# Nine quarters of the key projection inside the first three steps, and the opening loads on three queues

## The chip, the cores and the metric

One program on one core of a Trainium2 chip. The metric is the device time in microseconds (us); lower is better. The kernel before took 767.0, 773.41 and 774.11 us in three runs, median 773.41 us.

## The reference, cut to what matters

One post-norm decoder block over x of shape (32, 128, 256), float32: causal self-attention with 16 heads, a cross attention without softmax (rotated queries and keys, a decay mask), and a mixture of 8 experts of which each token uses two, with a shared expert. The part that this change touches is how the self-attention gets its keys:

```python
qkv = jnp.einsum('bsd,de->bse', x, qkv_weights).reshape(-1, 3 * D)
q = jnp.transpose(pre_q, (0, 2, 1, 3)).reshape(-1, S, Dh)
v = jnp.transpose(pre_v, (0, 2, 1, 3)).reshape(-1, S, Dh)
k = jnp.transpose(pre_k, (0, 2, 3, 1)).reshape(-1, S, Dh)   # k is reshaped across positions
a = jnp.einsum('aib,ajb->aij', q, k) / scale
a = jax.nn.softmax(tril * a + NEG_INF * (1.0 - tril), axis=-1)
x = _layernorm(x + heads)            # then cross attention, norm, experts, norm
```

The reshape of k mixes positions and channels, so the keys of a head aren't a slice of the projection: the kernel writes the projected keys to a DRAM tensor, k_dram, and reads them back in another order.

## The kernel before, in words

**The key projection.** x is 32 batches, taken as 4 groups of 8. For each group the projection of K comes in 4 quarters, so there are 16 quarters. A quarter (project_k, line 711) is four float32 products of 256 columns, eight records in the trace, into one PSUM bank; VectorE then copies the bank into first_use (out_k, line 1242). After four quarters SyncE stores the group, 1 MB, to k_dram (store_k, line 445). The rows of a group lie batch by batch: batch b of a group is 16 of the 128 partitions. Before the loop TensorE does 12 quarters (line 720), then waits for every load of the opening (lines 728 to 735); the last four come in steps 0 and 1 (lines 846 to 851 and 935 to 938), each behind a wait on kk_set, the count of copied quarters.

**The loop.** Each engine runs step(n) for n from -2 on, one batch further in each stage per step. In step n TensorE turns the probabilities of batch n-1 in four pieces (turn_probs, line 778), applies them to v of batch n-2 (weigh), makes the scores of batch n (scores, line 761), and projects q and v of batch n+1 (project, line 737). VectorE takes the row maxima (line 1259), lays the causal mask of two of the four score banks for the next batch (line 1365), and does the moments of the norms. ScalarE does the exponentials (line 1085), copies the turned probabilities out (line 1092), lays the other two masks (line 1097) and scales q (line 1149). Each engine does its own in the order written; semaphores order them against each other. scores(n) needs q, the four masks (near_laid, far_laid) and the keys of batch n (kp_in).

**SyncE's queue.** All loads of the opening are issued by SyncE in one row: wk (the K part of the weights), group 0 of x in four pieces, groups 1 to 3, the identity, the Q and V weights, and then load_small (line 435): gate and shared biases, the tables tf and tb (the mask is in tb), and the three cross attention weights. Then store_k(0), and in the loop per step: x for the next projection (line 470), the keys of batch n+1 in eight reads of 16 KB (line 480), one store_k, context and rows of x (lines 501, 505). In steps 3 to 6 it also loads the experts' weights into first_use (lines 488 to 497), ahead of the context of that step. GpSimd's queue writes zeros for idle rows to sent in step 2 (line 627), as soon as zeros is set.

## Time and profile before

| | |
|---|---|
| median of three runs | 773.41 us |
| the profiled execution, whole time | 769.79 us |
| its span, first to last instruction | 768.0 us |
| granted TensorE clock, mean over the span | 0.971 |
| TensorE busy | 702.7 us (92%) |
| first scores of the loop begin | 32.51 us into the span |

The profiled execution is one of its own. Its 769.79 us are the span and 1.8 us around it. Times of rows below count from the span's start. A row of the timeline gives start, duration, engine, line and operation, and in brackets how long the engine had been idle before it and what ended that. The profile's granted clock is 1.00 at TensorE's upper level (2.4 GHz) and 0.50 at its lower (1.2 GHz).

### The profile page before, as it was taken

What the parts mean: (1) busy time and instruction counts of PE and PEld (TensorE: products, weight loads), DVE (VectorE), ACT (ScalarE), POOL (GpSimd) and SP (SyncE); (2) the same over time, 40 slices, a digit from 0 to 9 for tenths busy, and PEclk for the clock granted to TensorE, in tenths of its full rate; (3) what the DMA queues carried; (4) which work ended last, traced back from release to release, by engine and by line L of the source; (5) the groups of instructions that cost most, each with busy time, mean ns of one, the idle gap of its engine ahead of it and who ended that gap; (6) DMA issues with size and microseconds to landing.
All of it is one profiled execution on the core that took longest, in us unless ns stands there. A gap on an engine that the chain in (4) does not pass through costs nothing.

```text
span 768.0 us, 19404 instructions
## 1 busy us (share of the span) xinstructions
PE 702.7 (92%) x5464; PEld 531.7 (69%) x5465; DVE 479.0 (62%) x1536; ACT 409.2 (53%) x1167; POOL 333.8 (43%) x483
## 2 busy tenths in 40 slices
PE   6977899999999999999987649999999999999993
PEld 5866788888888888888875315566666666665453
DVE  3555577888888888888865433444444444438984
ACT  0268688888888888888851102333333333312232
POOL 1002233345555555555565553555555555541111
PEclk9999999999999999999999768999999999999998
DMA  8745562223333332333371543322222222218962
GB/s 296 249 146 155 149 220 75 82 65 101 102 90 90 101 112 77 102 101 98 91 235 53 155 138 117 125 89 83 89 82 89 82 89 82 89 59 319 307 213 82
DMA packets 77032, 97.54 MB, mean 127 GB/s; under 512 B 12320, under 2 KB 63264, under 8 KB 75936
## 3 DMA queue, kind: packets, MB, share of 16 engines
q1 hardware_dynamic: 59920, 68.21, 28.5%
q0 software_dynamic: 6816, 19.00, 6.9%
q10 hardware_dynamic: 10224, 9.42, 4.6%
q8 instruction: 39, 0.64, 0.4%
q14 instruction: 33, 0.27, 0.1%
HBM read 60.02 MB, written 36.56 MB: 126 GB/s over the span
## 4 chain that ended last, share of the span: by engine, by line
PE 69%; issue 13%; DVE 4%; POOL 4%; SPq 4%; DMA 4%; ACT 1%; DVEq 0%; POOLq 0%; ACTq 0%
PE ps L996 16%; PE ps L1007 8%; PE ps L783 6%; PE ps L861 4%; PE ps L771 4%; PE ps L793 4%; PE ps L748 4%; PE ps L864 3%; PE ps L885 3%; PE ps L751 3%; DVE products L1269 3%; PE ps L982 2%; POOL sent L640 2%; PE ps L989 2%; PE ps L922 2%
## 5 line engine op out<-in xcount | busy, mean ns | idle before, releaser
L1085 ACT ACTIVATE prob<-ps,nmax 128x128 f32<-128x128 f32 x512 | 146.4, 377 | 29.1 <-DVE nmax L1259 29.0
L996 PE MATMUL ps<-first_use,xgT 128*128 x284 | 135.6, 600 | 1.5 <-ACT xgT L1190 1.5
L1489 DVE TENSOR_TENSOR hid<-ps,attn_only 128x512 f32<-128x512 f32 x71 | 49.1, 692 | 95.6 <-PE ps L996 94.4
L1190 ACT COPY xgT<-ps 128x256 f32<-128x256 f32 x71 | 26.4, 372 | 137.2 <-PE ps L982 137.2
L1259 DVE TENSOR_REDUCE nmax<-ps 128x4 f32<-128x512 f32 x128 | 82.2, 685 | 19.9 <-PE ps L771 18.5
L677 POOL TENSOR_TENSOR gate_h<-hid,sil 128x256 f32<-128x256 f32 x71 | 50.8, 715 | 96.6 <-DVE result_row L1502 83.0
L1092 ACT COPY pT<-ps 128x512 f32<-128x512 f32 x128 | 76.7, 599 | 18.9 <-PE ps L783 14.7
L783 PE MATMUL ps<-tf,prob 128*128 128x128 f32 x512 | 78.2, 275 | 5.7 <-ACT pT L1092 5.7
L996 PEld LDWEIGHTS ps<-first_use,xgT 128*128 128x128 f32 x284 | 54.3, 192 | 40.5 <-issue 37.0
L640 POOL DMA_INDIRECT sent<-packets,pos x64 | 63.7, 995 | 37.3 <-PE ps L771 22.8
L680 POOL DMA_INDIRECT back<-yg,result_row x71 | 71.5, 1007 | 14.3 <-issue 12.4
L1007 PE MATMUL ps<-first_use,ghT 128*128 x284 | 74.1, 384 | 0.5 <-ACT ghT L1195 0.5
L783 PEld LDWEIGHTS ps<-tf,prob 128*128 128x128 f32 x512 | 59.2, 141 | 11.8 <-issue 5.8
L801 PE MATMUL ps<-prob,sw_sb 128*128 128x512 f32 x128 | 62.7, 641 | 3.5 <-DMA prob<-x2T_dram 2.5
L647 POOL TENSOR_TENSOR res<-att,attn_only 128x256 f32<-128x256 f32 x32 | 23.4, 731 | 86.9 <-DVE att L1387 86.9
L1508 DVE TENSOR_TENSOR yg<-ps,attn_only 128x256 f32<-128x256 f32 x71 | 30.2, 425 | 41.7 <-PE ps L1007 37.6
L982 PEld LDWEIGHTS ps<-tf,xg 128*128 128x128 f32 x142 | 18.8, 143 | 52.3 <-issue 50.9
L621 POOL TENSOR_TENSOR rot<-products 128x128 f32<-128x128 f32 x128 | 54.2, 455 | 0.0
L1007 PEld LDWEIGHTS ps<-first_use,ghT 128*128 128x128 f32 x284 | 48.4, 190 | 4.9 <-issue 0.9
L1269 DVE TENSOR_TENSOR products<-ps,tf 128x256 f32<-128x256 f32 x128 | 46.3, 404 | 5.0 <-PE ps L864 1.1
L801 PEld LDWEIGHTS ps<-prob,sw_sb 128*128 128x128 f32 x128 | 25.7, 205 | 32.9 <-issue 29.5
L659 POOL TENSOR_TENSOR rstd<-mv,neg_half 128x1 f32<-128x1 f32 x32 | 17.6, 550 | 67.0 <-DVE mv L1277 67.0
(135 smaller groups left out, 1408.8 us busy)
## 6 DMA issues: line engine op xcount, KB each, us to landing
xg<-sent ACTq DMA_DIRECT2D x68, 129.5 KB, 2.1
first_use<-back SPq DMA_DIRECT2D x8, 1024.0 KB, 7.9
k_dram<-first_use SPq DMA_DIRECT2D x4, 1024.0 KB, 4.4
attn_only<-in_x_turned SPq DMA_DIRECT2D x32, 128.0 KB, 3.0
attn_only<-k_dram SPq DMA_DIRECT2D x256, 16.0 KB
attn_only<-in_x SPq DMA_DIRECT2D x32, 128.0 KB, 2.8
attn_only<-in_ctx SPq DMA_DIRECT2D x32, 128.0 KB, 2.9
first_use<-in_L_ffn_rw SPq DMA_DIRECT2D x8, 512.0 KB, 5.2
```

The lines of the kernel that those rows point to most:

```text
L621: eng.tensor_tensor(rot[:, t % 2, m + e, :], ra[:, t % 2, m + e, :], rb[:, t % 2, m + 1 - e, :], ALU.add).then_inc(done, 1)
L640: eng.indirect_dma_start(sent, bass.IndirectOffsetOnAxis(ap=pos[:, t, j:j + 1], axis=0), packets[:, t % SLOTS, :], None).then_inc(sent_in[ ...
L677: eng.tensor_tensor(gate_h[:, r, :], hid[:, r, FFN:2 * FFN], sil[:, r, :], ALU.mult).then_inc(gh_set, 1)
L680: eng.indirect_dma_start(back, bass.IndirectOffsetOnAxis(ap=result_row[:, slot:slot + 1], axis=0), yg[:, slot % 2, :], None).then_inc(yg_o ...
L783: mm = eng.transpose(PROBT[:, n * P:(n + 1) * P], prob[:, t % 2, 4 * u + n, :], ident)
L801: mm = eng.matmul(ps[:, bank0 + 2 * f + half, :].rearrange("p (b t) -> p b t", b=QB), sw1_sb[:, c, cols:cols + P], x2T4[:, r, :, c, :], st ...
L996: mm = eng.matmul(ps[:, r, :], xgT[:, r, c, :], rw1_sb[:, bass.ds(e * (DC * 2 * FFN) + c * 2 * FFN, 2 * FFN)], start=(c == 0), stop=(c == ...
L1007: mm = eng.matmul(ps[:, 4 + r, 0:D], ghT[:, r, c, :], rw2_sb[:, bass.ds(e * (FFN // P * D) + c * D, D)], start=(c == 0), stop=(c == FFN // ...
L1085: ins = eng.activation(prob[:, t % 2, 4 * u + n, :], SCORE[u][:, n * P:(n + 1) * P], ACT.Exp, bias=nmax[:, t % 2, 4 * u + n:4 * u + n + 1])
L1092: eng.copy(pT[:, u, :, :].rearrange("p n t -> p (n t)"), PROBT).then_inc(pT_set, 1)
L1259: eng.tensor_reduce(nmax[:, t % 2, 4 * u:4 * u + 4], SCORE[u].rearrange("p (h j) -> p h j", j=P), AX_X, ALU.max, negate=True).then_inc(max ...
L1269: eng.tensor_tensor(into[:, t % 2, m:m + 2, :], source, table[:, m:m + 2, :], ALU.mult).then_inc(done, 1)
```

## The change

What it does, by place:

- TensorE does quarters 0 to 3 first, then the projection of q and v of batch 0 and the masks, then quarters 4 to 6, then the first scores. Quarters 7 to 9 lie in step 0, 10 to 12 in step 1, 13 to 15 in step 2. A table, K_BANK, gives each quarter its PSUM bank. VectorE's copies follow (out_ks).
- The big wait ahead of the loop is split: tables and cross weights are waited for in step 3, the small ones in step 5.
- SyncE loads only the K weights, group 0, the Q and V weights, x for batches 0 and 1, tb and the identity. ScalarE's queue loads group 1 (when group 0 is in), group 2 (in step 0) and group 3 (behind its first four exponentials). GpSimd's queue does load_small, when group 1 is in.
- The store of group 0 is two stores: the 16 partitions of batch 0, and the other 112. Batch 0's keys are then read by SyncE (four reads) and ScalarE (four reads).
- Stores of groups 1 to 3 come at the end of SyncE's steps 0 to 2; experts' weights one step later (steps 4 to 7); the zeros in GpSimd's step 4.

```diff
 MAX_ORDER = (1, 0, 3, 2)
+K_BANK = (4, 5, 6, 7, 4, 5, 7, 4, 5, 7, 5, 7, 5, 7, 6, 7)
 PADDING = B * S * TOPK
...
         kk_set = sem("kk_set")
-        k_stored = [sem("k_stored_first"), sem("k_stored_rest")]
+        k_stored = [sem("k_stored_batch"), sem("k_stored_group"), sem("k_stored_rest")]
+        mask_in = sem("mask_in")
...
                               x_blocks[0, :, 2 * j:2 * j + 2].rearrange("p u n -> p (u n)")).then_inc(first_in[j], 16)
-            for g in range(1, NG):
-                eng.dma_start(xTu[g][:, :, :, :, :].rearrange("p u c b i -> p (u c b i)"),
-                              x_blocks[g].rearrange("p u n -> p (u n)")).then_inc(xTu_in[g], 16)
-            eng.dma_start(ident, table_f32[:, 0:P]).then_inc(ident_in, 16)
             for n in (0, 2):
                 eng.dma_start(wqkv_sb[:, :, n * D:(n + 1) * D], wqkv_rows[:, :, n * D:(n + 1) * D]).then_inc(w_in, 16)
-            def load_small():
-                eng.dma_start(gate_w_sb[:, :, :], gate_w.rearrange("(c p) n -> p c n", p=P)).then_inc(small_in, 16)
...
-                eng.dma_start(tb[:, :], table_bf16).then_inc(tables_in, 16)
-                for w, src in ((xwq_sb, xwq), (xwk_sb, xwk), (xwv_sb, xwv)):
-                    eng.dma_start(w[:, :, :], src.rearrange("(c p) n -> p c n", p=P)).then_inc(xw_in, 16)
+            eng.dma_start(xT[:, 0, :, :], x_turned[0]).then_inc(xT_in[0], 16)
+            eng.dma_start(tb[:, :], table_bf16).then_inc(mask_in, 16)
+            eng.dma_start(xT[:, 1, :, :], x_turned[1]).then_inc(xT_in[1], 16)
+            eng.dma_start(ident, table_f32[:, 0:P]).then_inc(ident_in, 16)
...
                 eng.wait_ge(kk_set, g * 4 + 4)
-                eng.dma_start(k_dram[g * GB:(g + 1) * GB].rearrange("b i g f -> (b i) (g f)"),
-                              kk_of(g)).then_inc(k_stored[min(g, 1)], 16)
-            load_small()
+                rows = k_dram[g * GB:(g + 1) * GB].rearrange("b i g f -> (b i) (g f)")
+                if g == 0:
+                    eng.dma_start(rows[0:DH, :], kk_of(g)[0:DH, :]).then_inc(k_stored[0], 16)
+                    eng.dma_start(rows[DH:P, :], kk_of(g)[DH:P, :]).then_inc(k_stored[1], 16)
+                else:
+                    eng.dma_start(rows, kk_of(g)).then_inc(k_stored[2], 16)
             store_k(0)
...
                 t = n + 2
-                if live(t):
+                if live(t) and t > 1:
                     after(eng, qv_made, t - 1)
...
                         eng.wait_ge(consts_set, 2)
-                    if t == 0:
-                        eng.wait_ge(k_stored[0], 16)
-                    for j in range(GB):
+                    if t < 2:
+                        eng.wait_ge(k_stored[t], 16)
+                    for j in range(GB if t else GB // 2):
                         lo = 16 * j
...
                                       k_dram[t, :, j, :]).then_inc(kp_in[t % 2], 16)
-                if n in (-1, 0, 1):
-                    store_k(n + 2)
-                if n == 3:
-                    eng.wait_ge(k_stored[1], 16 * (NG - 1))
-                if 2 < n <= 2 + NE // 2:
-                    if n == 3:
+                if n == 4:
+                    eng.wait_ge(k_stored[2], 16 * (NG - 1))
+                if 3 < n <= 3 + NE // 2:
+                    if n == 4:
                         eng.dma_start(sw1_sb[:, :, :], sw1[0].rearrange("(c p) n -> p c n", p=P)).then_inc(ffn_in, 16)
...
-                    for e in range(2 * (n - 3), 2 * (n - 2)):
+                    for e in range(2 * (n - 4), 2 * (n - 3)):
                         lo = e * DC * 2 * FFN
...
                     eng.dma_start(xn[:, t % 2, :], x[t]).then_inc(xn_in[t % 2], 16)
+                if n in (0, 1, 2):
+                    store_k(n + 1)
                 if n == B:
...
+            def load_small():
+                eng.dma_start(tf[:, P:], table_f32[:, P:]).then_inc(tables_in, 16)
+                for w, src in ((xwq_sb, xwq), (xwk_sb, xwk), (xwv_sb, xwv)):
+                    eng.dma_start(w[:, :, :], src.rearrange("(c p) n -> p c n", p=P)).then_inc(xw_in, 16)
+                eng.dma_start(gate_w_sb[:, :, :], gate_w.rearrange("(c p) n -> p c n", p=P)).then_inc(small_in, 16)
+                eng.dma_start(gate_b_sb[:, 0:NE], gate_b.rearrange("(o n) -> o n", o=1).broadcast_to([P, NE])).then_inc(small_in, 16)
+                eng.dma_start(sb1_sb[:, :], sb1[0].rearrange("(c p) -> p c", p=P), allow_slow_non_contiguous=True).then_inc(small_in, 16)
+                eng.dma_start(sb2_sb[:, :], sb2.broadcast_to([P, D])).then_inc(small_in, 16)
+            eng.wait_ge(xTu_in[1], 16)
+            load_small()
             def turn_into(t, m, made, done):
...
             def step(n):
-                if n == 2:
+                if n == 4:
                     eng.wait_ge(zeros_set, 1)
...
-            for g in range(NG - 1):
-                eng.wait_ge(xTu_in[g] if g else wk_in, 16)
-                for j in range(4):
-                    if g == 0:
-                        eng.wait_ge(first_in[j], 16)
-                    else:
-                        eng.wait_ge(kk_set, (g - 1) * 4 + j + 1)
-                    project_k(g, j, 4 + j)
-            eng.wait_ge(xTu_in[NG - 1], 16)
-            eng.wait_ge(ident_in, 16)
+            def project_ks(first, end):
+                for i in range(first, end):
+                    if i == 0:
+                        eng.wait_ge(wk_in, 16)
+                    if i < 4:
+                        eng.wait_ge(first_in[i], 16)
+                    elif i % 4 == 0:
+                        eng.wait_ge(xTu_in[i // 4], 16)
+                    if K_BANK[i] in K_BANK[:i]:
+                        eng.wait_ge(kk_set, i - K_BANK[:i][::-1].index(K_BANK[i]))
+                    project_k(i // 4, i % 4, K_BANK[i])
+            project_ks(0, 4)
             eng.wait_ge(w_in, 32)
-            eng.wait_ge(kk_set, 4 * NG - 5)
-            eng.wait_ge(tables_in, 32)
-            eng.wait_ge(xw_in, 48)
-            eng.wait_ge(small_in, 64)
+            eng.wait_ge(mask_in, 16)
             eng.wait_ge(consts_set, 2)
+            eng.wait_ge(kk_set, 3)
...
             def step(n):
+                if n == 0:
+                    project_ks(4, 7)
                 if n == 1:
-                    eng.wait_ge(kk_set, 13)
+                    eng.wait_ge(ident_in, 16)
+                    eng.wait_ge(kk_set, 8)
+                if n == 3:
+                    eng.wait_ge(tables_in, 16)
+                    eng.wait_ge(xw_in, 48)
+                if n == 5:
+                    eng.wait_ge(small_in, 64)
                 if live(n - 1):
...
                 if n == 2:
-                    eng.wait_ge(kk_set, 4 * NG)
+                    eng.wait_ge(kk_set, 13)
                 if live(n - 2):
...
                 if n == 0:
-                    eng.wait_ge(kk_set, 9)
-                    project_k(NG - 1, 0, 4)
+                    project_ks(7, 9)
                 if n == 1:
-                    eng.wait_ge(kk_set, 14)
-                    project_k(NG - 1, 3, 5)
+                    project_ks(10, 11)
+                if n == 2:
+                    project_ks(13, 14)
                 t = n - 3
...
                     turn_probs(n - 1, 1)
+                if n == 1:
+                    project_ks(11, 12)
                 t = n - 3
...
                     turn_probs(n - 1, 2)
+                if n == 1:
+                    project_ks(12, 13)
+                if n == 2:
+                    eng.wait_ge(q_set, 3)
+                    eng.wait_ge(v_set, 3)
+                    project_ks(14, 16)
                 t = n - 5
...
                     mm.then_inc(gate_made, 1)
+                if n == 2:
+                    eng.wait_ge(kk_set, 15)
                 if live(n + 1):
...
                 if n == 0:
-                    eng.wait_ge(kk_set, 12)
-                    project_k(NG - 1, 1, 5)
-                    project_k(NG - 1, 2, 7)
+                    project_ks(9, 10)
                 for q in groups_at(n, 3):
...
                     eng.wait_ge(x1_set, t + 1)
+                    if n == 2:
+                        eng.wait_ge(kk_set, 4 * NG)
                     after(eng, gc_set, n - 4)
...
+            def load_blocks(g):
+                eng.dma_start(xTu[g][:, :, :, :, :].rearrange("p u c b i -> p (u c b i)"),
+                              x_blocks[g].rearrange("p u n -> p (u n)")).then_inc(xTu_in[g], 16)
+            eng.wait_ge(first_in[3], 16)
+            load_blocks(1)
             def step(n):
+                if n == 0:
+                    load_blocks(2)
+                    eng.wait_ge(k_stored[0], 16)
+                    for j in range(GB // 2, GB):
+                        lo = 16 * j
+                        eng.dma_start(kp[lo:lo + DH, 0, j % 2, :, :].rearrange("p a u -> p (a u)"),
+                                      k_dram[0, :, j, :]).then_inc(kp_in[0], 16)
                 if live(n - 1):
...
                     exps(n, 1)
+                if n == 0:
+                    load_blocks(3)
                 for q in groups_at(n, 1):
...
         def _(eng):
-            def out_k(g, j, bank):
-                eng.wait_ge(k_made, g * 4 + j + 1)
-                eng.tensor_copy(kk_of(g).rearrange("p (a u) -> p u a", u=NU)[:, 2 * j:2 * j + 2, :],
-                                ps[:, bank, :].rearrange("p (u a) -> p u a", u=2)).then_inc(kk_set, 1)
-            for g in range(NG - 1):
-                for j in range(4):
-                    out_k(g, j, 4 + j)
-            eng.wait_ge(tables_in, 32)
-            eng.wait_ge(consts_set, 2)
-            eng.tensor_copy(base[:, :], region_rows).then_inc(base_set, 1)
-            eng.tensor_copy(zeros[:, D:PACKET], padding_end).then_inc(zeros_set, 1)
+            def out_ks(first, end):
+                for i in range(first, end):
+                    eng.wait_ge(k_made, i + 1)
+                    eng.tensor_copy(kk_of(i // 4).rearrange("p (a u) -> p u a", u=NU)[:, i % 4 * 2:i % 4 * 2 + 2, :],
+                                    ps[:, K_BANK[i], :].rearrange("p (u a) -> p u a", u=2)).then_inc(kk_set, 1)
+            out_ks(0, 4)
...
                 r2, r4 = t2 % 2, t4 % 2
+                if n == 0:
+                    out_ks(4, 7)
+                    eng.wait_ge(mask_in, 16)
+                    eng.wait_ge(consts_set, 2)
+                if n == 1:
+                    out_ks(9, 10)
                 if live(n):
...
                 if n == 0:
-                    for j, bank in enumerate((4, 5, 7)):
-                        out_k(NG - 1, j, bank)
+                    out_ks(7, 9)
                 if n == 1:
-                    out_k(NG - 1, 3, 5)
+                    out_ks(10, 12)
+                if n == 2:
+                    out_ks(13, 14)
                 if live(t2):
...
                                       rden[:, r2, :].unsqueeze(2).broadcast_to([P, H, DH]), ALU.mult).then_inc(att_set, 1)
+                if n == 2:
+                    out_ks(14, 15)
                 if live(t3):
...
                     lay_mask(n + 1, 3)
+                if n == 1:
+                    out_ks(12, 13)
+                if n == 2:
+                    out_ks(15, 16)
+                    eng.wait_ge(tables_in, 16)
+                    eng.tensor_copy(base[:, :], region_rows).then_inc(base_set, 1)
+                    eng.tensor_copy(zeros[:, D:PACKET], padding_end).then_inc(zeros_set, 1)
                 if live(t4):
```

TensorE's order from its first product to scores(1), before (714 is a quarter's product, four to a quarter; 748 and 751 the projection of q and v, 758 the masks, 771 the scores, 783 turned probabilities):

```order
L714 MATMUL ps<-attn_only,prob 128x256 x32
L714 MATMUL ps<-attn_only,first_use 128x256 x16
L748 MATMUL ps<-attn_only 128x128 x4
L751 MATMUL ps<-attn_only 128x256 x2
L758 MATMUL ps<-tb 128x512 x4
L771 MATMUL ps<-attn_only 128x128 x16
L714 MATMUL ps<-attn_only,first_use 128x256 x4
L748 MATMUL ps<-attn_only 128x128 x4
```

and now (721 is a quarter's product, 757 and 760 the projection, 767 the masks, 780 the scores, 792 turned probabilities; lines of the changed file):

```order
L721 MATMUL ps<-attn_only,prob 128x256 x16
L757 MATMUL ps<-attn_only 128x128 x4
L760 MATMUL ps<-attn_only 128x256 x2
L767 MATMUL ps<-tb 128x512 x4
L721 MATMUL ps<-attn_only,prob 128x256 x12
L780 MATMUL ps<-attn_only 128x128 x16
L721 MATMUL ps<-attn_only,prob 128x256 x4
L721 MATMUL ps<-attn_only,first_use 128x256 x4
L757 MATMUL ps<-attn_only 128x128 x4
L760 MATMUL ps<-attn_only 128x256 x2
L721 MATMUL ps<-attn_only,first_use 128x256 x4
L792 MATMUL ps<-tf,prob 128x128 x4
```

Twelve quarters stood ahead of the first scores and seven do now; the projection and the masks have moved in among them. Quarter 8, the first from first_use, needs group 2.

VectorE in step 2, from the maxima of batch 2 to the masks for batch 3, before (1365 is the mask, 1244 would be a quarter's copy):

```order
L1259 TENSOR_REDUCE nmax<-ps 128x4 [waits expd,scored] x3
L1382 RECIPROCAL rden<-ps 128x16 [waits heads_turned]
L1387 TENSOR_TENSOR att<-ps,rden 128x256 [waits den_set]
L1396 BN_STATS bn<-res 128x6 [waits res1_set]
L1273 BN_AGGR mv<-bn 128x2 [waits bn1_set]
L1277 TENSOR_SCALAR mv<-mv 128x1 [waits mv1_set]
L1259 TENSOR_REDUCE nmax<-ps 128x4 [waits expd,scored]
L1411 TENSOR_SCALAR x<-res,mv,rstd 128x256 [waits rstd1_set]
L1365 CAST ps<-tb 128x512 [waits expd] x2
```

and now (1288 is a quarter's copy, 1402 the mask):

```order
L1296 TENSOR_REDUCE nmax<-ps 128x4 [waits expd,scored] x3
L1288 COPY first_use<-ps 128x2x256 [waits k_made]
L1426 RECIPROCAL rden<-ps 128x16 [waits heads_turned]
L1431 TENSOR_TENSOR att<-ps,rden 128x256 [waits den_set]
L1288 COPY first_use<-ps 128x2x256 [waits k_made]
L1442 BN_STATS bn<-res 128x6 [waits res1_set]
L1310 BN_AGGR mv<-bn 128x2 [waits bn1_set]
L1314 TENSOR_SCALAR mv<-mv 128x1 [waits mv1_set]
L1296 TENSOR_REDUCE nmax<-ps 128x4 [waits expd,scored]
L1457 TENSOR_SCALAR x<-res,mv,rstd 128x256 [waits rstd1_set]
L1402 CAST ps<-tb 128x512 [waits expd] x2
L1288 COPY first_use<-ps 128x2x256 [waits k_made]
```

Three copies now lie in this step, the last behind both masks; TensorE's transposes of x1 (line 987 of the changed file), which stand at the end of its step 2, wait for that last copy.

## Rows read from the trace of the kernel before

**Rows 1.** The page: shares of the chain that ended last, by engine
```profile
PE 69%; issue 13%; DVE 4%; POOL 4%; SPq 4%; DMA 4%; ACT 1%; DVEq 0%; POOLq 0%; ACTq 0%
```

**Rows 2.** Timeline, 0 to 60 us, up to the first scores
```profile
5.78 16.49 PE L714 MATMUL ps<-attn_only,prob 128*128 128x256 f32 x64 [5.78 <-DMA prob<-in_x_blocks]
...
15.40 1.08 DVE L1244 COPY first_use<-ps 128x512 f32<-128x512 f32 x1 [0.65 <-PE ps L714]
17.12 1.08 DVE L1244 COPY first_use<-ps 128x512 f32<-128x512 f32 x1 [0.65 <-PE ps L714]
...
29.01 1.10 PE L748 MATMUL ps<-attn_only 128*128 128x128 f32 x8
...
30.81 1.03 PE L758 MATMUL ps<-tb 128*128 128x512 bf16 x4
...
32.51 1.17 PE L771 MATMUL ps<-attn_only 32*128 32x128 f32 x32 [0.67 <-DMA attn_only<-k_dram]
```

**Rows 3.** Chain that ended last, 0 to 80 us: start, duration, what
```profile
19.17 8.32 DMA k_dram<-first_use
...
30.73 1.64 DMA attn_only<-k_dram
...
71.16 7.78 DMA attn_only<-in_ctx
```

**Rows 4.** Stretches: start:end, length, each engine's busy us, granted clock, DMA share, GB/s
```profile
19.00:26.00 7.00, 7.00 (x35) 6.16 (x34) 4.43 (x5) 0.00 (x0) 0.00 (x0) 1.00 0.94 353
32.50:43.36 10.86, 8.74 (x72) 7.65 (x73) 6.82 (x9) 6.50 (x21) 0.00 (x0) 1.00 0.90 300
43.36:54.51 11.15, 9.61 (x101) 7.80 (x101) 4.85 (x7) 7.56 (x23) 0.00 (x0) 0.85 0.38 124
44.90:48.10 3.20, 3.20 (x10) 2.47 (x9) 2.30 (x5) 2.17 (x8) 0.00 (x0) 0.50 0.03 8
54.50:64.60 10.10, 6.85 (x102) 5.75 (x98) 5.52 (x12) 8.66 (x26) 1.30 (x2) 1.00 0.22 55
```

**Rows 5.** Timeline, steps 0 to 2: TensorE, VectorE, ScalarE
```profile
33.71 2.49 DVE L1259 TENSOR_REDUCE nmax<-ps 128x4 f32<-128x512 f32 x4 [3.36 <-PE ps L771]
...
41.77 1.34 DVE L1365 CAST ps<-tb 128x512 f32<-128x512 bf16 x2
...
43.36 1.17 PE L771 MATMUL ps<-attn_only 32*128 32x128 f32 x32 [2.12 <-DVE ps L1365]
...
54.51 1.18 PE L771 MATMUL ps<-attn_only 32*128 32x128 f32 x32
...
59.26 0.63 PE L783 MATMUL ps<-tf,prob 128*128 128x128 f32 x4 [2.34 <-ACT pT L1092]
...
63.56 0.60 ACT L1097 CAST ps<-tb 128x512 f32<-128x512 bf16 x1
...
64.64 1.17 PE L771 MATMUL ps<-attn_only 32*128 32x128 f32 x32
```

**Rows 6.** Timeline: SyncE's and GpSimd's DMA issues, 31 to 68 us
```profile
31.04 1.15 POOL L627 DMA_DIRECT2D sent<-zeros  x1 [27.50 <-DVE zeros L1254]
31.19 0.42 SPq L447 DMA_DIRECT2D k_dram<-first_use  x1
...
32.13 6.79 SPq L480 DMA_DIRECT2D attn_only<-k_dram  x8
...
63.44 4.64 SPq L480 DMA_DIRECT2D attn_only<-k_dram  x8
```

**Rows 7.** Line 447, the four stores of K, issue to landing
```profile
DMA to landing us min/median/max: 4.2/4.4/8.3
```

**Rows 8.** Line 429, loads of groups 1 to 3, issue to landing
```profile
DMA to landing us min/median/max: 8.1/10.1/12.2
```

**Rows 9.** Timeline of TensorE: context products of batch 0 and of batch 1
```profile
65.74 1.16 PE L861 MATMUL ps<-attn_only 128*128 128x128 f32 x8
...
78.98 2.08 PE L861 MATMUL ps<-attn_only 128*128 128x128 f32 x8 [2.60 <-DMA attn_only<-in_ctx]
```

More of the change, by code:

```diff
@@ L427, in _ @@
                               x_blocks[0, :, 2 * j:2 * j + 2].rearrange("p u n -> p (u n)")).then_inc(first_in[j], 16)
-            for g in range(1, NG):
-                eng.dma_start(xTu[g][:, :, :, :, :].rearrange("p u c b i -> p (u c b i)"),
-                              x_blocks[g].rearrange("p u n -> p (u n)")).then_inc(xTu_in[g], 16)
-            eng.dma_start(ident, table_f32[:, 0:P]).then_inc(ident_in, 16)
             for n in (0, 2):
                 eng.dma_start(wqkv_sb[:, :, n * D:(n + 1) * D], wqkv_rows[:, :, n * D:(n + 1) * D]).then_inc(w_in, 16)
-            def load_small():
-                eng.dma_start(gate_w_sb[:, :, :], gate_w.rearrange("(c p) n -> p c n", p=P)).then_inc(small_in, 16)
-                eng.dma_start(gate_b_sb[:, 0:NE], gate_b.rearrange("(o n) -> o n", o=1).broadcast_to([P, NE])).then_inc(small_in, 16)
-                eng.dma_start(sb1_sb[:, :], sb1[0].rearrange("(c p) -> p c", p=P), allow_slow_non_contiguous=True).then_inc(small_in, 16)
-                eng.dma_start(sb2_sb[:, :], sb2.broadcast_to([P, D])).then_inc(small_in, 16)
-                eng.dma_start(tf[:, P:], table_f32[:, P:]).then_inc(tables_in, 16)
-                eng.dma_start(tb[:, :], table_bf16).then_inc(tables_in, 16)
-                for w, src in ((xwq_sb, xwq), (xwk_sb, xwk), (xwv_sb, xwv)):
-                    eng.dma_start(w[:, :, :], src.rearrange("(c p) n -> p c n", p=P)).then_inc(xw_in, 16)
```

## The prediction, as it was made

> **What bounds the kernel now.** The page comes first: TensorE makes up 69% of the chain of work that ended last [rows 1], so a microsecond that TensorE loses at the start is lost at the end, and one that it gains there is gained, as long as the steps behind it keep their pace. The timeline of the opening is next [rows 2]. TensorE starts on the quarters of K at 5.78 us; VectorE's copies of quarters 3 and 4 start 1.72 us apart (15.40 and 17.12), and that is the pace of a quarter. The projection of q and v for batch 0 starts at 29.01 us, behind twelve quarters, the masks end at 31.84, and the first scores start at 32.51 after 0.67 us of waiting for keys. The chain of waits shows a second path that is almost as long: the store of group 0, issued at 19.17 although its last copy ended at 16.48 (15.40 plus 1.08), takes 8.32 us, and the last key read issued at 30.73 takes 1.64 us more [rows 3]. TensorE's queue and the DMA path end within 0.7 us of each other, so a change has to shorten both.
>
> Then the steps. Between the first scores and 64.6 us TensorE isn't full [rows 4]: it is idle for 2.12 us in the first of the three stretches (10.86 less 8.74), 1.54 in the second, 3.25 in the third, 6.9 together. The gap of 2.12 us stands ahead of scores(1) and ends with VectorE's mask [rows 5]. About 1.5 us after it the granted clock is at the lower of its two levels, 1.2 GHz, from 44.9 to 48.1 us [rows 4]; 3.2 us at half rate cost 1.6. A gap of 2.34 us at 59.26 [rows 5] has no such fall behind it: that stretch is at 1.00 throughout [rows 4].
>
> **What the change can win at most.** TensorE does the same sixteen quarters. The gain can only be idle time or low clock that goes away: 0.67 + 6.9 + 1.6 = 9.2 us up to scores(3), which stand at 64.64 us [rows 5].
>
> **The first scores.** TensorE: quarter 3 is made at 15.4, the projection and the masks take 2.8 us (29.01 to 31.84, of which the projection 1.8) [rows 2], three quarters 5.2, so TensorE is ready at 23.4. Group 1 for quarter 4 is needed at 18.2; in the trace it landed 8.1 us after its issue at 3.2 us, behind 1.3 MB [rows 8]. It now starts some 5 us later with about 1 MB beside it, and should be in by 14: no cost.
>
> The keys: the store of batch 0's 16 partitions can start at 16.5 to 16.9, since load_small no longer stands ahead of it (2.7 us of issue before). Its landing is not in the trace; the bounds are 1.64 us, the key read, and 8.3, the slowest of the 1 MB stores [rows 3, 7], with 4.2 for an undisturbed 1 MB store. I take 3, between the small read and that 4.2: 19.6. Four reads on each queue need 1.4 us to the last issue, 21.0. Their landing has the bounds 1.64 and 7.78, the latter the context read behind a row of bulk loads [rows 3]. Here they stand behind the other 0.9 MB of group 0's store on one queue and behind 1 MB of group 2 on the other, while GpSimd's loads drain. In flight from 17.5 on are about 0.9 + 1.05 + 0.8 MB; at 353 GB/s, the rate of the stretch from 19 to 26 us in which the DMA engines were 94% busy [rows 4], that is 7.8 us, to 25.3. I take 4 us for the reads: first scores at **25.0**, TensorE idle for 1.6 us ahead of them.
>
> The Trainium skill (DMA: Bandwidth & Descriptors, Issuing engines are not separate DMA queues) says that loads issued from several engines run on the same 16 DMA engines, and that spreading them saves only the issue time. Taken alone it would leave the keys where the bytes put them and give this part only the 2.7 us of earlier issue; the 0.94 share agrees with it. The order of the bytes, which the change also turns, is outside that rule.
>
> **Steps 0 to 2.** Step 0 has the same work on TensorE as before (scores, three quarters, the projection, one turned piece), 8.74 us [rows 4]. VectorE has the scores' 1.2, four maxima (2.5), two copies (2.2) and two masks (1.3) [rows 5], and ends 7.2 after the scores began; before, a third copy stood ahead of the masks, and it had to wait for its quarter. ScalarE with its extra issues needs about 8. So scores(1) at 33.7, with no gap where 2.12 us were. Step 1 had 9.61 busy [rows 4]; less 1.6 for the low clock and 1.7 for its one quarter that is 6.3, with three quarters, 5.2, it is 11.5, less a few tenths that each piece's end overlaps with the next once no gap stands between them: 10.8. The quarters lie in the places where TensorE waited for ScalarE's copies. scores(2) at 44.5. Step 2: 6.85 of work [rows 4] plus three quarters, 5.2, is 12.0; two waits stay. The third turned piece waits about 1 us for ScalarE (the same place had 2.34, of which quarter 13 now covers the rest). At the end, x1 is transposed only when quarter 15 has been copied, and that copy of 1.08 stands behind both masks on VectorE; ScalarE then needs 0.4 for x1, 0.6 for its own mask [rows 5] and 0.4 for q before scores(3). In the old order TensorE's project ran into this point; now it waits about 1.3. Step 2 is 14.3, scores(3) at 58.8 against 64.64: 5.8 us. The other way of counting, 9.2 less the 1.6, 1.0 and 1.3 that wait now, is 5.3. I take **5.6**.
>
> VectorE's mask no longer makes TensorE wait, and I expect no low clock in step 1: 1.6 of the 5.6 are that.
>
> **What comes later.** Experts' weights move from step 3 to step 4. They cost a stall: the context of batch 1 is read behind them and lands 7.78 us after its issue [rows 3], TensorE waits 2.60 us and then runs slowly (2.08 us for products that take 1.16 elsewhere) [rows 9]. The same queue order one step later gives the same stall one step later: nothing gained or lost. New beside it are the zeros (0.93 MB) on GpSimd's queue, which start in step 4 as soon as GpSimd is free. In the trace, the eight key reads issued next to zeros and a store took 6.79 us, in step 3 without either 4.64 [rows 6]. So the context comes 0 to 2.15 us later; I take 0.9, as the zeros start some microseconds ahead of the reads. SyncE's store of group 3 now makes it wait in step 2 for quarter 15, about 2 us past the moment at which it would have loaded x for batch 5; that load is not needed for a step: no cost, and if the cover went it would be 2 us. VectorE's two small copies, 0.3 us, lie ahead of a wait. Nothing else moves.
>
> **The sum.** 5.6 less 0.9 is 4.7 us. Against the profiled execution that is 769.8 - 4.7 = 765.1; that execution is 3.6 us under the median of 773.4, which would give 768.7. The three runs and the profiled one average 771.1, so neither is typical; I forecast **767**. About 1%, 7.7 us, is what a measurement of this kernel can tell from no change.
>
> **Rivals.**
> - *The keys are early* (0.20). The store lands in 2 us and the reads behind it in 2: first scores at 23.4, TensorE never waits. Then 5.6 + 1.6, and 0.3 more if the zeros cost little: 7.5, about 764. For it: batch 0's store is an eighth of a group. Against it: the busy DMA engines.
> - *The bytes decide* (0.20). All three queues drain together and the keys land at 28; TensorE is idle for 4.6 us and, as behind the 2.12 us gap, runs at the low clock afterwards: 3.0 and 1.6 lost, gain about 0, 771.
> - *Group 2 is late* (0.09). It is issued at about 18.2, when ScalarE has q and v of batch 0, and quarter 8 wants it at 27.8. If it lands after the longest time seen, 12.2 us [rows 8], it comes at 30.4: 2.6 us lost, gain 2, 769.
> - *Slower* (0.06). Batch 0's store stands behind GpSimd's 1.6 MB as group 0's store stood behind the same loads, 8.3 us, so 25.2; the reads then take 7.78: first scores at 34.4, against 32.51. This turns the sign from 30.6 on (25.0 + 5.6). Price: 9.4 less 5.6, and 1.6 for the clock, 5.4 slower, 777. Against it: those loads are on another queue now.
>
> **Chances.** The forecast itself has 0.45, with a range of its own of 764 to 770. Faster by over 1%: all of the first rival and about 0.12 of the forecast's, whose base may as well be the 770 of the profile: 0.32. Slower by over 1%: 0.06. Within 1%: 0.62. Range: 761 takes in the early keys, 773 the bytes' case and the scatter between runs (767.0 to 774.1); what is left out is the slow rival and the ends of the scatter.
>
> **What the new profile would show.** First scores near 25 us, ahead of them a gap of 1 to 2 us that ends with a DMA (over 4: the bytes; none: early keys). scores(1), (2), (3) near 33.7, 44.5, 58.8. Granted clock 1.00 through step 1; 0.50 behind the first scores would cost 1.6. In step 2 a gap ahead of the turned x1, ended by VectorE's copy of quarter 15; if it isn't there, the gain at scores(3) is 7. In step 5 a gap of 2.6 to 4.7 ended by the context's DMA; if it is gone, the forecast is 4 us too high. From step 6 on each step as before.

## The result, and the profile after

The changed kernel takes 774.31 us (median of 22 runs, 768.0 to 777.98), the kernel before on the same chip 769.74 (22 runs, 765.41 to 775.24). The ratio is 1.0055, with a 95% interval of 1.0035 to 1.0075: by this ratio 4.2 us slower, where 4.7 us less were forecast. The profiled execution of after took 772.58 us, with a span of 770.8, against the 768.0 of before.

The opening of the changed kernel, from its timeline (start, duration, engine, line, operation, tiles; in brackets the idle time ahead of it and what ended it):

```profile
14.25 0.77 POOL L612 DMA_DIRECT2D tf<-in_table_f  x1 [10.71 <-DMA prob<-in_x_blocks]
16.24 0.34 SPq L441 DMA_DIRECT2D k_dram<-first_use  x1
16.62 0.42 SPq L442 DMA_DIRECT2D k_dram<-first_use  x1
16.89 0.35 ACTq L1127 DMA_DIRECT2D first_use<-in_x_blocks  x1
...
21.61 2.01 ACTq L1139 DMA_DIRECT2D attn_only<-k_dram  x4
21.66 1.91 SPq L475 DMA_DIRECT2D attn_only<-k_dram  x4
30.05 2.09 PE L780 MATMUL ps<-attn_only 32*128 32x128 f32 x32 [7.17 <-DMA attn_only<-k_dram]
...
40.49 1.17 PE L780 MATMUL ps<-attn_only 32*128 32x128 f32 x32
51.49 1.17 PE L780 MATMUL ps<-attn_only 32*128 32x128 f32 x32
```

TensorE is ready for the first scores 9.0 us earlier than in [rows 2], at 22.9 instead of 31.84 us, but the keys let the first scores start only at 30.05, 2.5 us earlier than before. The batch's store is issued at 16.24, and the reads, which wait for it, start at 21.6. The table of DMA issues from 14 to 30 us (tile, queue, transfers, KB, median us from issue to landing) shows how long everything in flight then takes:

```profile
first_use<-in_x_blocks ACTq DMA_DIRECT2D x1, 1024.0 KB, 11.4
k_dram<-first_use SPq DMA_DIRECT2D x1, 896.0 KB, 10.5
tf<-in_table_f POOLq DMA_DIRECT2D x1, 705.0 KB, 4.7
k_dram<-first_use SPq DMA_DIRECT2D x1, 128.0 KB, 5.3
```

Group 2's 1 MB needs 11.4 us where the fastest store of that size took 4.2 [rows 7]. The chain of waits has the store and the last read one behind the other:

```profile
16.24 5.34 DMA k_dram<-first_use
23.16 6.76 DMA attn_only<-k_dram
...
84.14 7.78 DMA attn_only<-in_ctx
```

The stretches of the opening (start:end, length, busy time of PE, PEld, DVE, ACT, POOL, then granted clock, DMA share, GB/s), to be read against [rows 4]:

```profile
17.00:21.50 4.50, 4.50 (x23) 3.78 (x21) 1.38 (x2) 0.53 (x2) 2.75 (x5) 1.00 0.99 331
21.50:27.00 5.50, 1.39 (x7) 0.88 (x5) 1.85 (x2) 0.00 (x0) 0.00 (x0) 1.00 1.01 373
27.00:30.00 3.00, 0.00 (x0) 0.00 (x0) 0.00 (x0) 0.00 (x0) 0.00 (x0) 0.50 0.40 95
30.00:33.20 3.20, 3.15 (x35) 2.77 (x36) 0.92 (x2) 0.19 (x1) 0.00 (x0) 0.50 0.10 24
33.20:33.80 0.60, 0.60 (x3) 0.51 (x2) 0.60 (x2) 0.60 (x4) 0.00 (x0) 0.50 0.00 0
```

The DMA engines are full for ten microseconds, 3.5 MB in 17 to 27 us, and fall to 95 GB/s just before the keys are in. The clock is at 1.2 GHz from 27.0 to 33.8 us; the scores take 2.09 us in place of 1.17. Step 0, from these scores to the next, takes 10.44 us (30.05 to 40.49) for work of 8.74 us [rows 4], with no gap: the low clock costs 1.7 us.

Steps 2 and 5, later in TensorE's timeline:

```profile
63.78 0.41 PE L987 MATMUL ps<-tf,x 128*128 128x128 f32 x2 [1.26 <-DVE first_use L1288]
65.59 1.17 PE L780 MATMUL ps<-attn_only 32*128 32x128 f32 x32
...
91.96 2.08 PE L878 MATMUL ps<-attn_only 128*128 128x128 f32 x8 [3.78 <-DMA attn_only<-in_ctx]
103.55 1.17 PE L780 MATMUL ps<-attn_only 32*128 32x128 f32 x32
```

scores(3) start at 65.59 against 64.64 [rows 5]: +1.0 us. The wait for batch 1's context is 3.78 us against 2.60 [rows 9], so scores(6) are at 103.55 against 101.47: +2.1. The last batch's scores are at 383.05 against 380.79, +2.3, and the spans differ by 2.8.

### The profile page after: what moved, and what is told of

It reads as the page before. It is cut to its first block, busy times and chain, and to the rows that moved or that the text cites. A ratio compares the mean times of both kernels' runs of the same rounds, so it can differ in the third digit from the quotient of the medians.

```text
span 770.8 us, 19409 instructions
## 1 busy us (share of the span) xinstructions
PE 702.1 (91%) x5464; PEld 531.3 (69%) x5465; DVE 478.2 (62%) x1536; ACT 410.0 (53%) x1167; POOL 339.3 (44%) x491
## 4 chain that ended last, share of the span: by engine, by line
PE 70%; issue 14%; DVE 5%; POOL 4%; DMA 4%; SPq 1%; ACT 1%; ACTq 0%; POOLq 0%; DVEq 0%
PE ps L1023 16%; PE ps L1034 8%; PE ps L792 5%; PE ps L780 5%; PE ps L878 4%; PE ps L802 4%; PE ps L757 4%; PE ps L881 3%; PE ps L904 3%; PE ps L760 3%; PE ps L721 3%; DVE products L1306 3%; PE ps L1009 2%; POOL sent L647 2%; PE ps L1016 2%
## 5 line engine op out<-in xcount | busy, mean ns | idle before, releaser
L654 POOL TENSOR_TENSOR res<-att,attn_only 128x256 f32<-128x256 f32 x32 | 23.4, 730 | 97.9 <-DVE att L1431 97.9
L1009 PEld LDWEIGHTS ps<-tf,xg 128*128 128x128 f32 x142 | 18.8, 143 | 53.1 <-issue 51.7
```

## The experiments

Each kernel is `after` with the edit shown, except the one built on `before`. A ratio is to the kernel before, timed on the same chip. The chips differ (the kernel before has medians from 769.7 to 776.4 us on them), and so do two openings of the same code, so rows of different traces are compared only roughly.

**Which of the three bulk transfers holds the keys.** First, GpSimd's loads wait for the keys:

```diff
-            eng.wait_ge(xTu_in[1], 16)
+            eng.wait_ge(kp_in[0], 128)
             load_small()
```

> The changed kernel, with GpSimd's 1.6 MB of tables and weights loaded only when batch 0's keys are in. Theory 1 (the keys land when the bytes queued on the 16 DMA engines ahead of them have drained): 1.6 MB less at 373 GB/s is 4.3 us, so the first scores come near 26 us instead of 30.05, with no or less low clock behind them, and the kernel takes 4 to 6 us less than the changed one, about 769 to 771. Rival (the reads of freshly stored keys are slow by themselves, whatever else is in flight): first scores stay at 29 to 30, time unchanged near 774.

Second, group 2 is issued right behind group 1:

```diff
             load_blocks(1)
+            load_blocks(2)
             def step(n):
                 if n == 0:
-                    load_blocks(2)
```

> The changed kernel, with group 2 loaded by ScalarE's queue right behind group 1, into the quiet stretch from 11 to 17 us (221 and 86 GB/s) instead of at 16.9 us. Theory 1: 1.05 MB less beside the keys, 2.8 us: first scores near 27.2, 3 to 4 us less than the changed kernel. Rival: first scores at 29 to 30, time as the changed kernel.

Third, the rest of group 0 is stored behind SyncE's four reads of batch 0:

```diff
                 if g == 0:
                     eng.dma_start(rows[0:DH, :], kk_of(g)[0:DH, :]).then_inc(k_stored[0], 16)
-                    eng.dma_start(rows[DH:P, :], kk_of(g)[DH:P, :]).then_inc(k_stored[1], 16)
...
+                if n == -1:
+                    rows = k_dram[0:GB].rearrange("b i g f -> (b i) (g f)")
+                    eng.dma_start(rows[DH:P, :], kk_of(0)[DH:P, :]).then_inc(k_stored[1], 16)
```

> The changed kernel, with the store of group 0's other 112 partitions (0.92 MB) issued behind SyncE's four reads of batch 0's keys. Theory 1: SyncE's four reads land 3 us or more sooner, ScalarE's four still stand behind group 2 on their own queue but with less traffic beside them: first scores at 27.5 to 29. Batch 1's keys come later by some 5 us and may then hold up scores(1). Rival: no change of the first scores.

The fourth kernel has all three edits.

> All three together: GpSimd's loads behind batch 0's keys, group 2 right behind group 1, the rest of group 0's store behind batch 0's reads. Theory 1: nothing large is in flight when the keys are stored and read; store lands in 2 to 3 us, reads in 2, TensorE hardly waits: first scores at 22.9 to 24.5, granted clock 1.00 behind them, scores(3) at 57 to 58.5, about 763 to 765, 9 to 10 us less than the changed kernel and 5 to 6 less than before. Rival: first scores later than 27.

Measured, with the first scores' row from each timeline. GpSimd's loads held back:

```profile
28.12 2.09 PE L780 MATMUL ps<-attn_only 32*128 32x128 f32 x32 [5.37 <-DMA attn_only<-k_dram]
```

Group 2 early:

```profile
29.95 2.09 PE L780 MATMUL ps<-attn_only 32*128 32x128 f32 x32 [6.80 <-DMA attn_only<-k_dram]
```

The rest's store behind the reads:

```profile
28.09 1.17 PE L782 MATMUL ps<-attn_only 32*128 32x128 f32 x32 [3.80 <-DMA attn_only<-k_dram]
```

All three, the first scores and those of batch 1:

```profile
22.45 1.17 PE L782 MATMUL ps<-attn_only 32*128 32x128 f32 x32
...
35.96 1.73 PE L782 MATMUL ps<-attn_only 32*128 32x128 f32 x32 [4.76 <-issue]
```

One edit alone gives 1.9, 0.1 and 2.0 us; the three together give 7.6, and there the keys are no longer what TensorE waits for. The single steps are close to the scatter: a second profile of the same opening, in the experiment on the zeros below, has its first scores at 31.42 instead of 30.05. A steadier measure is the time from the issue of batch 0's store to the first scores. The changed kernel takes 13.8 us for it (16.24 to 30.05), and 14.9 in that second profile; the single edits take 12.0, 13.5 and 10.5 (their stores are issued at 16.10, 16.50 and 17.64), and all three together 6.75 (from 15.70). So the third edit is worth more than its 2.0 us show. By this measure the three parts sum to 5.5 us of 7.1 against the first profile and to 8.7 of 8.1 against the second, so whether they simply add up can't be told. No run left just one of the three transfers in place. Of the expected first scores (26, 27.2, and 27.5 to 29) only the third came true, and the fourth kernel's scores(3), expected at 57 to 58.5, came later.

With group 2 early, group 1 landed at 15.65 instead of 13.57 and GpSimd's loads started at 16.34 instead of 14.25. In the second profile of the opening they start at 16.30 without such an edit, so this shift isn't shown to be the edit's work; against that profile, group 2 early gains 1.5 us.

Ratios: 1.0025 (0.9987 to 1.0063), 1.0008 (0.9973 to 1.0043), 0.9961 (0.9919 to 1.0004), and for all three 0.9997 (0.9964 to 1.0031). The third alone lies wholly below the changed kernel's 1.0035 to 1.0075. All three together show no gain over the kernel before, for two reasons. First, the delay moved: the keys of batch 1 now stand behind the same bytes. Its SyncE queue and its stretches:

```profile
20.89 0.42 SPq L478 DMA_DIRECT2D k_dram<-first_use  x1
25.93 4.19 SPq L474 DMA_DIRECT2D attn_only<-k_dram  x8
```

```profile
28.00:32.00 4.00, 3.19 (x18) 2.60 (x16) 2.66 (x4) 2.99 (x9) 0.50 (x1) 1.00 1.03 400
32.00:36.00 4.00, 0.04 (x4) 0.07 (x4) 0.00 (x0) 0.00 (x0) 0.00 (x0) 1.00 0.99 315
```

Its scores(3) are at 62.67, 2.9 us earlier than after's, where its first scores are 7.6 earlier, but still 2.0 earlier than before's. Second, these 2.0 go at the context, where the wait is longer than the 2.60 us of [rows 9]: its scores(6) are at 101.51, level with before's 101.47.

```profile
88.77 2.08 PE L880 MATMUL ps<-attn_only 128*128 128x128 f32 x8 [3.51 <-DMA attn_only<-in_ctx]
```

**The bulk behind the keys of batch 1 too.** The fourth kernel, with GpSimd's loads behind batch 1's keys and group 3 loaded later in ScalarE's step 0:

```diff
-            eng.wait_ge(kp_in[0], 128)
+            eng.wait_ge(kp_in[1], 128)
             load_small()
...
-                if n == 0:
-                    load_blocks(3)
...
+                if n == 0:
+                    load_blocks(3)
                 if live(n) and live(n + 1):
                     lay_mask(n + 1, 2)
```

> As the kernel with everything behind batch 0's keys, but the large loads now also stand behind batch 1's keys: GpSimd's 1.6 MB start when batch 1's keys are in, and ScalarE issues group 3 at the end of its step 0. Theory 1 (bytes ahead of a key read set when it lands; the 4.8 us wait ahead of scores(1) there is the same effect one batch on): scores at 22.4, 31 to 32, 42 to 43, 56 to 57.5; granted clock 1.00 up to there; 5 to 7 us less than before, ratio about 0.992. Rival (the rest of group 0's store and the 8 reads behind it take this long by themselves, since only 5 us lie between them): scores(1) still at 35 to 36, ratio 0.998 to 1.0.

```profile
34.35 1.17 PE L782 MATMUL ps<-attn_only 32*128 32x128 f32 x32 [1.57 <-issue]
...
34.94 0.77 POOL L614 DMA_DIRECT2D tf<-in_table_f  x1 [31.40 <-DMA attn_only<-k_dram]
...
85.29 2.08 PE L880 MATMUL ps<-attn_only 128*128 128x128 f32 x8 [3.25 <-DMA attn_only<-in_ctx]
```

Ratio 0.9927 (0.9893 to 0.9961), by it 5.7 us faster than before. GpSimd, which waits for batch 1's keys alone, starts right behind scores(1): they are what the 1.57 us were spent on. The bulk isn't wholly behind them even here, as group 3's load is issued at 27.90 and group 1's store at 30.74. Its scores(3) start at 59.45, 5.2 us ahead of before's 64.64, and its scores(6) at 97.94, 3.5 ahead, the difference being lost at the context; 3.5 is inside the interval. Here a gain of the start arrives in the total. Its scores(3) are 0.65 us behind the 58.8 forecast for the change: its first scores, at 24.03 with no wait, are 1.0 earlier than the forecast 25.0, and the wait at scores(1) takes 1.57.

**The zeros and the context.** First the zeros alone, moved to step 9:

```diff
-                if n == 4:
+                if n == 9:
                     eng.wait_ge(zeros_set, 1)
```

> The changed kernel, with the zeros written in GpSimd's step 9 instead of step 4. If the zeros beside the key reads of step 4 lengthen the wait for the context: that wait falls from 3.78 to 2.6 us, 1 to 1.5 us less than the changed kernel, first scores still at 30, ratio to before about 1.003. Rival (the wait is longer only because the step order on SyncE's queue shifted): wait stays at 3.5 to 4.

Its first scores, its context products, and SyncE's eight key reads of step 4:

```profile
31.42 2.09 PE L780 MATMUL ps<-attn_only 32*128 32x128 f32 x32 [8.22 <-DMA attn_only<-k_dram]
...
92.54 1.16 PE L878 MATMUL ps<-attn_only 128*128 128x128 f32 x8 [1.87 <-DMA attn_only<-in_ctx]
```

```profile
77.46 4.60 SPq L475 DMA_DIRECT2D attn_only<-k_dram  x8
```

The reads' issues take 4.60 us instead of 5.75, and the context wait is 1.87 instead of 3.78, with no low clock behind it; in the other six profiles above and below that keep the zeros and the order of the change's step 4, the wait is 3.17 to 4.23. Step 5 is 3.5 us shorter. The first scores came at 31.42 though nothing was edited ahead of them: GpSimd's loads started 2.05 us later here, and the keys' landing differs by 1.4 us between two profiles of one opening. With the low clock behind it (to 37.5 us) this puts scores(3) 2.5 us later than after's, so scores(6), at 102.55, are 1.0 earlier. The ratio is 0.9995 (0.9965 to 1.0024), 4.6 us below the changed kernel's; this profile accounts for 1.0 of them, and the rest stays open.

Then the fifth kernel, with the zeros in step 9 and SyncE's context and x loads moved ahead of the experts' weights:

```diff
+                t = n - 2
+                if live(t):
+                    after(eng, xkv_made, t - 1)
+                    eng.dma_start(cT[:, t % 2, :, :], ctx_turned[t]).then_inc(cT_in[t % 2], 16)
...
                 if 3 < n <= 3 + NE // 2:
...
-                    eng.dma_start(cT[:, t % 2, :, :], ctx_turned[t]).then_inc(cT_in[t % 2], 16)
```

> As the previous with all bulk behind batch 1's keys, the zeros in step 9, and SyncE's context and x rows issued ahead of the experts' weights in steps 4 to 7. If the wait in step 5 is only the context standing behind 2.25 MB of weights in the same queue: no wait there, no low clock behind it, step 5 takes 11.1 us instead of 16.5, and together with the early keys the kernel takes 10 to 12 us less than before, ratio about 0.986. Rival (the weights delay the next keys instead, which stand behind them then): a wait of 2 us or more ahead of scores(6) or (7), ratio 0.99 to 0.995.

```profile
32.59 1.17 PE L782 MATMUL ps<-attn_only 32*128 32x128 f32 x32 [1.43 <-issue]
...
55.89 0.41 PE L989 MATMUL ps<-tf,x 128*128 128x128 f32 x2 [1.26 <-DVE first_use L1290]
...
80.22 1.16 PE L880 MATMUL ps<-attn_only 128*128 128x128 f32 x8
```

No context wait is left, and the clock stays high. Median 767.35 us, ratio 0.9879 (0.9834 to 0.9924): by it 9.4 us faster than before on that chip. Its last batch's scores start at 371.58, 9.2 us earlier than in before's trace, which is of another chip.

**The old order with an earlier store.** `before`, with load_small alone moved to GpSimd's queue, behind group 1:

```diff
             store_k(0)
-            load_small()
...
+            eng.wait_ge(xTu_in[1], 16)
+            load_small()
```

> The kernel before, with one part of the change alone: the small loads and tables issued by GpSimd when group 1 is in, instead of by SyncE ahead of the first store of K. TensorE still does twelve quarters, the projection and the masks first. Theory (the two paths to the first scores have nearly the same length, so shortening the DMA path alone brings 0.7 us at most): store of group 0 issued at 16.5, first scores at 31.8 to 32.3 without a wait, time the same as before within 1 us. Rival (the DMA path is what bounds): first scores before 30, gain 2 us or more.

```profile
16.07 0.34 SPq L437 DMA_DIRECT2D k_dram<-first_use  x1
26.92 3.62 SPq L469 DMA_DIRECT2D attn_only<-k_dram  x8
```

The store is issued 3.1 us earlier than in [rows 3], takes 10.77 us instead of 8.32 and is done 0.65 us earlier; the loads' bytes still run beside it. The first scores are at 31.91 against 32.51. More couldn't be won there, as TensorE is ready only at 31.6: in the old order the two paths do end together, as the prediction said. Ratio 0.9973 (0.9939 to 1.0007).

**A queue of their own for the keys.** The rest's store and group 2 are issued by GpSimd ahead of its loads, so that SyncE's and ScalarE's queues hold nothing ahead of batch 0's reads but its store:

```diff
             eng.wait_ge(xTu_in[1], 16)
+            eng.wait_ge(kk_set, 4)
+            rows = k_dram[0:GB].rearrange("b i g f -> (b i) (g f)")
+            eng.dma_start(rows[DH:P, :], kk_of(0)[DH:P, :]).then_inc(k_stored[1], 16)
+            eng.dma_start(xTu[2][:, :, :, :, :].rearrange("p u c b i -> p (u c b i)"),
+                          x_blocks[2].rearrange("p u n -> p (u n)")).then_inc(xTu_in[2], 16)
             load_small()
```

> The changed kernel with the same bytes in flight beside batch 0's keys, but none of them in the two queues that read the keys: the store of group 0's other 112 partitions and the load of group 2 are issued by GpSimd, ahead of its 1.6 MB, once group 1 is in and quarter 3 copied (about 16.5 us). SyncE's and ScalarE's queues hold only batch 0's store and reads. Theory A (a key read waits for the bulk ahead of it in its own queue; across queues the engines take turns): batch 0's store lands in 3 to 5.5 us, the reads in 2 to 3: first scores at 22.5 to 25. Theory B (only the sum of bytes in flight counts, whichever queue): 3.6 MB at 0.35 MB per us from 16.5 are through at 27, first scores at 27 to 30 as in the changed kernel. Group 2 and batch 1's keys may come later than in the changed kernel, so no gain in time is promised by either.

```profile
16.16 0.34 SPq L441 DMA_DIRECT2D k_dram<-first_use  x1
18.89 2.90 SPq L474 DMA_DIRECT2D attn_only<-k_dram  x4
27.71 2.09 PE L784 MATMUL ps<-attn_only 32*128 32x128 f32 x32 [4.91 <-DMA attn_only<-k_dram]
```

```profile
17.00:21.50 4.50, 4.50 (x22) 3.87 (x21) 1.47 (x2) 0.45 (x2) 4.50 (x7) 1.00 0.99 237
21.50:27.00 5.50, 1.30 (x7) 0.80 (x5) 1.77 (x2) 0.00 (x0) 1.95 (x4) 0.95 1.00 374
```

What each queue moved (packets, MB, share of the 16 DMA engines' time; q0 is GpSimd's, q1 SyncE's, q10 ScalarE's), from 18.8 to 22.5 us and then from 27.7 to 32 us:

```profile
q0 software_dynamic: 156, 1.15, 86.9%
```

```profile
q0 software_dynamic: 301, 0.63, 57.0%
```

The store now lands in 2.7 us instead of 5.3 (4.2 in the second profile of that opening), and the first scores come 2.3 us earlier. But the reads, issued from 18.84 and 18.89 on with their queues empty ahead of them, take as long as in the changed kernel: 8.9 us from the first issue to the first scores, where that takes 8.4 (21.61 to 30.05) and the kernel with all three edits 3.35 (19.10 to 22.45). Until 22.5 us not one packet of theirs moved, while GpSimd's queue moved 1.15 MB. So bulk ahead of them in their own queue isn't needed to hold the reads; bulk on a third queue does it as well. Nor do they wait for all of it: 0.63 MB of GpSimd's are moved after the keys are in. The ratio is 1.001 (0.9978 to 1.0042). The Trainium skill (DMA: Bandwidth & Descriptors, Issuing engines are not separate DMA queues) says that loads issued from several engines run on the same 16 DMA engines, interleaved, and that only issue time is saved. The 0.65 us of the run before agree. Here the reads gained nothing by their empty queues either; that no packet of theirs moved for the first 3.6 us is more than the section tells.

**Quarter 15's copy ahead of the mask.** The context-first kernel, with VectorE's copy of quarter 15 moved in step 2:

```diff
+                if n == 2:
+                    out_ks(15, 16)
                 lay_mask(n + 1, 0)
```

> As the kernel with all bulk late and the context first, with VectorE's copy of quarter 15 ahead of both masks of step 2 instead of behind them. If that copy's place is what holds x1's transposes (1.26 us of waiting): the wait falls to 0 to 0.3, scores(3) 0.8 to 1.2 us earlier, ratio to before about 0.987. Rival (the masks, now later, hold scores(3) instead): scores(3) unchanged.

```profile
33.42 1.17 PE L782 MATMUL ps<-attn_only 32*128 32x128 f32 x32 [1.79 <-issue]
...
55.55 0.41 PE L989 MATMUL ps<-tf,x 128*128 128x128 f32 x2
...
57.35 1.17 PE L782 MATMUL ps<-attn_only 32*128 32x128 f32 x32
```

The wait ahead of the turned x1 is gone, and step 2 takes 12.9 us (44.4 to 57.35) instead of 14.1. Median 760.28 us against 769.85 of before, ratio 0.9876 (0.9835 to 0.9916). This is the fastest version run, but its ratio can't be told from that of the kernel it is built on (0.9879); that the 1.2 us reach the end is shown by no timing.

## Why the prediction was wrong

- **What bounds the kernel**: right. Two paths of nearly equal length, TensorE's queue and the keys' DMA path, and both had to be shortened. The change shortened the first by 9.0 us and the second by 2.5.
- **TensorE ready at 23.4**: right (22.9). Group 1 landed at 13.57, by 14 as forecast.
- **The landing of batch 0's keys: the step that failed.** The store was taken at 3 us and took 5.3. The reads were taken at 4 us from the last issue at 21.0; that issue came at 23.16, and they took 6.8. First scores 30.05, not 25.0: 5.05 us. The sum of bytes in flight had two faults. It had half of GpSimd's loads through by 17.5 us. In the trace they are issued from 14.25 on, but from 14 to 17 us the DMA engines move only 86 GB/s, and 3.5 MB, not 2.75, are moved from 17 to 27. And it let the keys come at 25.0 as a part of the bytes, before the last of them at 25.3; in the trace the keys came last. Both prices were inside their bounds, picked from the low half. The kernels with all three transfers held back (first scores at 22.45, and in the three built on it at 22.42 to 24.03, never with a wait) show that these bytes are the cause; with one of the three removed, 10.5 to 13.5 of 13.8 us are left between the store's issue and the first scores. How far they do it in the reads' own queues and how far across queues stays partly open, as said below.
- **The clock behind it**: "no low clock in step 1" was right for step 1. But the wait of 7.17 us brought 1.2 GHz in its place, from 27.0 to 33.8. It cost 1.7 us, about the 1.6 at which the prediction priced it in its bytes-decide rival.
- **Steps 0 to 2**: right. Step 0 took 10.44 us, which is 8.74 and the clock's 1.7, without a gap. Step 1 took 11.0 (10.8), step 2 14.1 (14.3), with a wait of 1.26 us ahead of the turned x1 (1.3), whose removal in the last run gave 1.2 back. The forecast 58.8 for scores(3), 5.05 for the keys and 1.7 for the clock make 65.55; measured were 65.59.
- **The context's stall and the zeros**: right in mechanism. 3.78 against 2.60 is 1.2 us; forecast was 0.9. With the zeros elsewhere it was 1.87, less than the 2.60 that were to be left; why is open.
- **Group 2 late**: didn't decide. It was issued at 16.89 and took 11.4 us, but TensorE was waiting for keys at 28.3 anyway.
- **The rival "the bytes decide"** (0.20) was the mechanism: keys at 28 and low clock behind. It was 2 us too early, and its 771 lay on a base of 767 + 4.7, 2 us above the 769.74 that 22 runs of before gave. "Slower" had the right sign by a store of 8.3 us that didn't occur; the sign did turn close to the stated 30.6, at 30.05, since the clock's loss had been left out of that point. With it the point was 29.0, and with the context's 0.9 as well 28.1.
- **The total**: of the +2.1 at scores(6), 1.0 are there at scores(3) and 1.2 come with the longer wait for the context. Of the 4.2 us, 0.2 more are there by the last scores and 0.5 in stages that the change doesn't touch; the other 1.4 lie between the profiled pair's spans and the medians, and stay open.

Also open is how the 16 DMA engines share themselves out. With GpSimd's loads held back, DMA moved only 84 GB/s from 24 to 28 us, yet the keys came at 28.12, 1.3 us behind group 2:

```profile
24.00:28.00 4.00, 0.00 (x0) 0.00 (x0) 0.00 (x0) 0.00 (x0) 0.00 (x0) 0.87 0.29 84
```

There group 2 was ahead of four of the reads in ScalarE's queue. A queue's order may add something, then, as may the 2.6 us that the store gained in a queue without bulk; neither was tried apart.

## What to carry to other kernels

When a small transfer ends the critical path, count every byte in flight on all queues at its issue, and price it as landing behind most of them: moving it to an empty queue of its own didn't speed up the reads, holding back the bulk did. Hold back all of it, past the next small transfer as well, or the wait moves one step on (of 7.6 us won at the first scores, 2.9 were left at scores(3) until batch 1's keys went first too, and the context's wait took 2 more). When TensorE is made ready much earlier than its input, the wait can cost twice: its length, and the low clock behind it. And before a step of 1 or 2 us in a trace is put down to an edit, look at a second trace of the same stretch: here two of them differ by 1.4 us.

## What the runs showed of the hardware

- Reads of 16 KB took 6.8 us from the last issue to landing beside 3.5 MB of bulk. From their first issue to the first scores it was 8.4 us; with their queues otherwise empty 8.9 (18.84 to 27.71), and with no bulk ahead of them 3.35.
- Two transfers of 0.9 and 1 MB side by side with 1.6 MB more took 10.5 and 11.4 us; [rows 7] has 4.2 for one.
- TensorE waits of 8.22, 7.17, 6.80, 5.37 and 4.91 us ahead of the first scores had 1.2 GHz behind them at once (scores of 2.09 us), as had the 3.78 us ahead of the context products (2.08). The wait of 3.80 us in the third kernel had it a little later: its scores ran at 1.17, and the stretch behind them was at 0.51. Waits of 1.43 to 1.87 us had none. Between them it goes both ways: there is a low clock behind 2.12 and 2.60 us in the trace of before and behind 3.25 in the fifth kernel, but none behind 2.34 [rows 5, 9] and none behind the third kernel's wait for the context of 3.17 us (granted clock 1.00 from 89.31 to 99.32). The length of a wait of 2 to 3 us alone doesn't tell.

```profile
30.00:33.00 3.00, 3.00 (x9) 2.34 (x8) 2.19 (x5) 2.87 (x11) 0.00 (x0) 0.51 0.60 188
```

The third kernel's context products:

```profile
89.31 1.16 PE L880 MATMUL ps<-attn_only 128*128 128x128 f32 x8 [3.17 <-DMA attn_only<-in_ctx]
```
